# The first two batches of an attention kernel: clearing the key tiles with ScalarE, dropping four small transfers, splitting a weight semaphore

## Chip, cores and metric

The kernel runs on one core of one Trainium2 chip. The metric is the device time of one execution in microseconds (us); the number before the change is the median of three runs.

## What is computed

One cross-attention layer and one routed feed-forward layer, in float32:

```python
# x: (32, 256, 256), ctx: (32, 120, 256), 16 heads of 16
q = split(layernorm(x) @ Wq); k = split(ctx @ Wk); v = split(ctx @ Wv)
attn = softmax(q k^T * 16 ** -0.5)
x = x + (attn v) @ Wp + bp
# y = layernorm(x); each of 16 experts takes the 512 tokens with its highest router logit
xn = rmsnorm(y) * norm_weight
logits = xn @ router_weight.T + router_bias
idx = top_k(logits.T, 512)
h = gelu(xn[idx] @ fc1.T + b1); yo = h @ fc2.T + b2
out = x + (sum of gate * yo over experts) / (sum of gates)
```

## The kernel before

The program has an attention phase (32 batches, about the first 465 us) and a routed phase (the rest). The change touches the attention phase alone, and in it only what is done once, ahead of the loop or in its first steps.

**Attention phase.** Each of the five engines has a program of its own, built by a function `step(i, c)` and unrolled for the first steps, looped for the middle ones and unrolled for the last (`run`). In one step, different batches stand at different stages: an offset `off` in `batch(i, c, off)` names which. Batch b's keys, rows and queries are computed in step b-2, its row maxima in step b-1, its scores and weighted values in step b, its projection later. Semaphores join the engines; `wait_ge` on one stops all that stands behind it on that engine. The order of instructions on an engine is the order in which the code is written.

**Tiles for the exact products.** Queries and keys are split into a high and a low part (QH, QL, KH, KL), which are moved by DMA, interleaved by partition, into the wide tiles `QX[u]` and `KX[u]` (u is the batch's parity). One partition in 64 (`MAX_ROW` = 3 in each half) is the row that brings in the maxima: in QX it holds zeros first (from `no_max`) and later the negated row maxima (`NMT`), and in KX it holds ones. All partitions that no transfer writes must be zero. So before batch 0 and 1 both QX and both KX are cleared, and the two rows of ones in each KX are set.

**Who does that now.** VectorE clears `QX[0]` (L521) ahead of normalising the rows of batch 0 (L524, `first_rows`), and `KX[0]` (L527) behind it. GpSimd clears `QX[1]` and `KX[1]` (L362, L363, `zeros`) after it has computed the `rstd` of batch 0 (L342, L344). All four raise the one semaphore `zeros_ready`. GpSimd also fills `ones` (L331), and four transfers on SyncE's DMA queue (L219) copy it into the rows of KX; SyncE issues them only when `zeros_ready` has all four, and everything behind them on SyncE (the load of x for batch 2, then the transfers of `no_max`, KL, KH and QL of batch 0) waits too. TensorE's first row maxima (`max_scores`, L745) wait for `kx_moved`, `qx_moved` and `ones_moved`.

**TensorE at the start.** It multiplies the identity 12 times (`warm_up`, L664) while the weights come in, computes the keys of batch 0 (L688), transposes its rows (L674), computes its queries (L716), multiplies the identity 12 times more, and goes on with the keys of batch 1, the values of batch 0 (L731) and the row maxima. The queries of batch 0 wait for `w_loaded` at 16 * 7, which is all of wq, wv, wp, bp, nw, rw and rb.

Of the kernel before, what the change touches and what calls it, by code (L numbers as in the profile page):

```python
# [16 lines left out]
M = 120  # L17
# [21 lines left out]
NX = HN * HALVES  # L39
NCONST = 7  # L40
GMAX = float(CAP) - 0.5
ROUNDS = 8
CLOCK = 16
WARM = 12
ALONE = 2
# [3 lines left out]
FIRST_W1, FIRST_W2, SECOND_W1 = 3, 8, 20  # L49
FE = 2  # L50


# [8 lines left out]
def attention_phase(nc, ctx, sem, bank, ident, L, search_tiles, search_consts, x, ctxT, wq, wk, wv, wp, bp, nw, rw, rb, out, xn_table):  # L61
# [19 lines left out]
    no_max = sb("no_max", [H, S], FP32)  # L81
    ones = sb("ones", [1, H * M // HALVES], FP32)

# [42 lines left out]

    wk_loaded, w_loaded = sem("wk_loaded"), sem("w_loaded")
    x_loaded = [sem(f"x_loaded{u}") for u in range(2)]
# [6 lines left out]
    max_moved = [sem(f"max_moved{u}") for u in range(2)]  # L135
    ones_moved = sem("ones_moved")
    oc_moved, rc_moved = sem("oc_moved"), [sem(f"rc_moved{g}") for g in range(KD)]
    pool_const, zeros_ready, search_const = sem("pool_const"), sem("zeros_ready"), sem("search_const")
    stats1_a, stats1_ready = sem("stats1_a"), sem("stats1_ready")
# [18 lines left out]
    pool_passed, dve_passed, sp_passed = sem("pool_passed"), sem("dve_passed"), sem("sp_passed")  # L158
    CONSTS = 4

# [5 lines left out]
    def known(b):  # L166

        return isinstance(b, int)
# [26 lines left out]
    def _(sp):  # L195
# [9 lines left out]
        load_ctx(0, 0)  # L205
        for t, w, loaded in ((wk_sb, wk, wk_loaded), (wq_sb, wq, w_loaded), (wv_sb, wv, w_loaded), (wp_sb, wp, w_loaded)):
            sp.dma_start(t[:, :, :], w.rearrange("(k p) c -> p k c", p=P)).then_inc(loaded, 16)
# [6 lines left out]
        sp.wait_ge(pool_const, NCONST)  # L214
        sp.wait_ge(zeros_ready, CONSTS)
        for u in range(2):
            for f in range(HALVES):
                row = HP * f + MAX_ROW
                sp.dma_start(KX[u][row:row + 1, :, f, :, :].bitcast(FP32).rearrange("p n e m -> p n (e m)"),  # L219
                             ones[:, :].rearrange("p (n r) -> p n r", n=HN)).then_inc(ones_moved, 16)  # L220

# [5 lines left out]
        def step(i, c):  # L227
# [15 lines left out]
            def clear_maxima():  # L243
                b, u, j, live = batch(i, c, -2)
                if live:
                    hold(score_done, NX * (b - 1))
                    if known(b) and b < 2:
                        hold(zeros_ready, CONSTS)
                    sp.dma_start(QX[u][MAX_ROW:P:HP, :, :].bitcast(FP32), no_max[:, :]).then_inc(qx_moved[u], 16)
# [8 lines left out]
            def keys(term, part, ready):  # L258
                b, u, j, live = batch(i, c, -2)
                if live:  # L260
                    hold(ready, b + 1)
                    hold(score_done, NX * (b - 1))
                    if known(b) and b == 0:
                        hold(zeros_ready, CONSTS)
                    for f in range(HALVES):
                        sp.dma_start(KX[u][HP * f + term:HP * (f + 1):4, :, f, :, :].bitcast(FP32).rearrange("p n e m -> p n (e m)"),
                                     part[u][HP * f:HP * (f + 1), :, :].bitcast(FP32).rearrange("p e m -> p (e m)")) \
                            .then_inc(kx_moved[u], 16)
# [55 lines left out]
    def _(pool):  # L324
        pool.memset(ident[:, :], 0.0).then_inc(pool_const, 1)
        pool.wait_ge(pool_const, 1)
        pool.affine_select(out=ident[:, :], in_=ident[:, :], compare_op=ALU.not_equal, fill=1.0, base=0,
                           pattern=[[-1, P]], channel_multiplier=1).then_inc(pool_const, 1)
        pool.memset(minus_half[:, :], -0.5).then_inc(pool_const, 1)
        pool.memset(no_max[:, :], 0.0).then_inc(pool_const, 1)  # L330
        pool.memset(ones[:, :], 1.0).then_inc(pool_const, 1)  # L331
        for u in range(2):
            pool.memset(VA[u][:, :, :, :], 1.0).then_inc(pool_const, 1)
        pool.wait_ge(pool_const, NCONST)

        def step(i, c):
# [23 lines left out]

            def zeros():
                pool.memset(QX[1][:, :, :].bitcast(FP32), 0.0).then_inc(zeros_ready, 1)  # L362
                pool.memset(KX[1][:, :, :, :, :].bitcast(FP32), 0.0).then_inc(zeros_ready, 1)  # L363

            def rows1():
                b, u, j, live = batch(i, c, -2)
                if known(b) and b == 0:
                    zeros()
                elif live:
# [12 lines left out]
            def residual():  # L382
                b, u, j, live = batch(i, c, 1)
                if live:
                    if known(b) and b == 0:
                        pool.wait_ge(w_loaded, 16 * 7)
# [20 lines left out]
    @block.scalar  # L407
    def _(act):
        act.wait_ge(pool_const, NCONST)
        act.activation(warm[:, :], minus_half[:, 0:1], ACT.Exp)  # L410

        def step(i, c):
# [43 lines left out]
            def move_high(off, term):  # L456

                b, u, j, live = batch(i, c, off)
                if live:
                    act.wait_ge(qh_ready, b + 1)  # L460
                    if known(b) and b < 2:
                        act.wait_ge(zeros_ready, CONSTS)
# [18 lines left out]
            def rows2():  # L481
                b, u, j, live = batch(i, c, 3)
                if live:
                    act.wait_ge(xn2T_done, b + 1)
                    wait(act, logit_done, b - 1)
                    if known(b) and b == 0:
                        act.wait_ge(w_loaded, 16 * 7)
# [29 lines left out]
    @block.vector  # L517
    def _(dve):
        def step(i, c):
            def first_rows():  # L520
                dve.memset(QX[0][:, :, :].bitcast(FP32), 0.0).then_inc(zeros_ready, 1)  # L521
                dve.wait_ge(rstd1_ready, 1)
                for t in range(TB):
                    ins = dve.tensor_scalar(XN[0][:, t, :], X[0][:, t, :], mv1[0][:, t, 0:1], rstd1[0][:, t:t + 1],  # L524
                                            ALU.subtract, ALU.mult)
                ins.then_inc(xn_ready, 1)
                dve.memset(KX[0][:, :, :, :, :].bitcast(FP32), 0.0).then_inc(zeros_ready, 1)  # L527

# [131 lines left out]
    def _(pe):  # L660
# [5 lines left out]
        pe.wait_ge(pool_const, 2)  # L666
        warm_up(WARM)
        pe.wait_ge(wk_loaded, 16)

        def step(i, c):  # L670
# [63 lines left out]
            def max_scores(q):  # L734
                b, u, j, live = batch(i, c, -1)
                if live:
                    t, n = q // HN, q % HN
                    if q == 0:
                        if known(b) and b == 0:
# [105 lines left out]

            last = 2 * i + c - (B - 1) if known(i) else -B
            maxima()
            if last == 2:
# [5 lines left out]
            scores(1)  # L854
            values()
            scores(2)
            max_scores(0)
# [15 lines left out]
            max_scores(5)  # L873
            first = 2 * i + c if known(i) else 0
            if first != -1:
# [3 lines left out]
            if first == -1:  # L879
                queries()  # L880
            if first == -2:
                warm_up(WARM)
            weigh(2)
# [927 lines left out]
```

## Time and profile before

| what | value |
|---|---|
| median of 3 runs | 980.95 us (980.31 to 984.34) |
| the profiled execution's own time | 983.5 us |
| its span, first to last instruction | 981.8 us |
| PE, DVE, ACT, POOL busy | 861.1, 747.0, 505.8, 591.7 us |
| PE's share of the span | 88% |

PE is TensorE (PEld its weight loads), DVE VectorE, ACT ScalarE, POOL GpSimd, SP SyncE; SPq and ACTq are DMA instructions issued by SP and ACT. A float32 matmul leaves two records in the trace, so counts of PE are twice those of the program there. PEclk is the clock granted to TensorE, where 1.00 is 2.4 GHz and 0.50 is 1.2 GHz.

### The profile page before, as it was taken

To read this page: it belongs to the slowest core of one execution; us is meant where nothing else is said; L and a number is where in the kernel's file an instruction comes from. 1 tells how busy PE (TensorE), PEld (TensorE's weight loads), DVE (VectorE), ACT (ScalarE), POOL (GpSimd) and SP (SyncE) were. 2 spreads that over 40 slices of the span, in tenths; PEclk is the share of its full clock that TensorE was granted. 3 is DMA by queue.
4 is the path that set the end of the run, shared out by engine and by line. 5 is a ranking of instruction groups with operands and counts; after the bars stand their busy time and mean duration, and the time that the engine had idled before them with its cause. 6 is when DMAs were issued, how large, how long until landed. Compare 5 with 4: busy or idle time off the path is not lost. (4 is left out here: it accounts for less than half of the span.)

```text
span 981.8 us, 20963 instructions
## 1 busy us (share of the span) xinstructions
PE 861.1 (88%) x6115; PEld 737.1 (75%) x6115; DVE 747.0 (76%) x1660; ACT 505.8 (52%) x921; POOL 591.7 (60%) x564
## 2 busy tenths in 40 slices
PE   7899999999999999998711149999999999999995
PEld 6678887888788887886510037989999999999985
DVE  4488888888888888887388965898777777777642
ACT  1356556655566556655256206465555555555531
POOL 4256667666676667665442264688876776775344
PEclk8799999999999999999755559999999999999998
DMA  5266666666566656654232033366766555665333
GB/s 161 92 202 226 207 207 206 213 219 208 192 212 222 207 204 205 212 193 157 75 103 83 3 88 127 113 196 181 183 162 157 159 155 161 161 175 153 85 70 43
DMA packets 129540, 156.51 MB, mean 159 GB/s; under 512 B 22464, under 2 KB 104656, under 8 KB 129376
## 3 DMA queue, kind: packets, MB, share of 16 engines
q1 hardware_dynamic: 104096, 113.06, 35.5%
q0 software_dynamic: 15616, 25.70, 12.1%
q10 hardware_dynamic: 9792, 17.31, 4.8%
q8 instruction: 17, 0.28, 0.1%
q14 instruction: 19, 0.16, 0.1%
HBM read 74.93 MB, written 26.28 MB: 103 GB/s over the span
## 5 line engine op out<-in xcount | busy, mean ns | idle before, releaser
L587 DVE TENSOR_REDUCE NM<-bank 128x4 f32<-128x480 f32 x256 | 155.4, 649 | 59.9 <-PE bank L745 59.9
L418 ACT ACTIVATE PT<-bank 120x512 f32<-120x512 f32 x256 | 142.8, 603 | 35.9 <-PE bank L770 34.7
L349 POOL TENSOR_SCALAR XN<-X,mv,rstd 128x256 f32<-128x256 f32 x124 | 150.5, 1222 | 14.1 <-POOL rstd L344 13.3
L1658 PE MATMUL bank<-W2H,HH 128*128 128x256 f32 x512 | 145.5, 284 | 2.0 <-issue 2.0
L1660 PE MATMUL bank<-W2H,HL 128*128 128x256 f32 x512 | 144.3, 282 | 0.0
L1659 PE MATMUL bank<-W2L,HH 128*128 128x256 f32 x512 | 144.3, 282 | 0.0
L1119 POOL DMA_INDIRECT out_dram<-C,IO x60 | 109.6, 1827 | 52.2 <-issue 31.3
L1387 DVE TENSOR_TENSOR HL<-hf,HH 128x512 fp32r<-128x512 f32 x128 | 87.5, 691 | 49.8 <-ACT HH L1542 49.3
L545 DVE RECIPROCAL RR<-RC 128x256 f32<-128x256 f32 x64 | 111.6, 1743 | 8.6 <-DMA RC<-PVS 8.6
L770 PE MATMUL bank<-QX,KX 128*120 128x256 f32 x512 | 110.8, 309 | 8.2 <-DMA QX<-NMT 5.0
L1537 ACT ACTIVATE hf<-bank,B 128x512 f32<-128x512 f32 x128 | 87.8, 686 | 40.9 <-PE bank L1660 35.6
L342 POOL TENSOR_SCALAR ve<-mv 128x2 f32<-128x2 f32 x64 | 12.2, 191 | 159.4 <-DVE mv L535 156.7
L745 PE MATMUL bank<-KX,QX 128*128 128x240 f32 x512 | 103.0, 304 | 5.2 <-DMA QX<-QL 2.1
L1658 PEld LDWEIGHTS bank<-W2H,HH 128*128 128x128 f32 x512 | 97.3, 190 | 3.1 <-issue 2.4
L1658 PE MATMUL bank<-XTH,W1H 128*128 128x512 f32 x240 | 96.3, 401 | 2.9 <-DVE XTL L1380 2.9
L1659 PEld LDWEIGHTS bank<-W2L,HH 128*128 128x128 f32 x512 | 97.2, 190 | 0.6
L1660 PEld LDWEIGHTS bank<-W2H,HL 128*128 128x128 f32 x512 | 97.1, 190 | 0.0
L1530 ACT ACTIVATE W2H<-W 128x2048 fp32r<-128x2048 f32 x15 | 28.8, 1920 | 131.9 <-PE bank L1660 131.9
L1660 PE MATMUL bank<-XTH,W1L 128*128 128x512 f32 x240 | 95.1, 396 | 0.0
L1659 PE MATMUL bank<-XTL,W1H 128*128 128x512 f32 x240 | 95.0, 396 | 0.0
L745 PEld LDWEIGHTS bank<-KX,QX 128*128 128x128 f32 x512 | 76.5, 192 | 23.0 <-DVE NM L587 15.4
L1096 POOL DMA_INDIRECT XG<-xn_table,II x64 | 72.6, 1135 | 33.0 <-DVE out_row L1312 16.8
(194 smaller groups left out, 1906.6 us busy)
## 6 DMA issues: line engine op xcount, KB each, us to landing
QX<-QH ACTq DMA_DIRECT2D x64, 256.0 KB
W<-w1T_dram SPq DMA_DIRECT2D x16, 1024.0 KB, 5.3
W<-w2T_dram SPq DMA_DIRECT2D x16, 1024.0 KB, 5.9
X<-x_dram SPq DMA_DIRECT2D x32, 256.0 KB, 3.0
QX<-QL SPq DMA_DIRECT2D x32, 256.0 KB
XB<-x_dram SPq DMA_DIRECT2D x32, 256.0 KB, 2.8
RC<-PVS SPq DMA_DIRECT2D x64, 128.0 KB, 2.1
OC<-PVS SPq DMA_DIRECT2D x64, 128.0 KB, 2.2
```

The lines of the kernel that those rows point to most:

```text
L349: ins = pool.tensor_scalar(dst[:, t, :], src[:, t, :], mv[:, t, 0:1], rstd[:, t:t + 1], ALU.subtract, ALU.mult)
L418: act.activation(PT[u][0:M, HE * k:HE * (k + 1), :], score_bank(b, k // 2)[k % 2][0:M, :], ACT.Exp, scale=SCALE) \
L545: dve.reciprocal(RR[:, g, :], RC[:, g, :]).then_inc(rr_ready, 1)
L587: dve.tensor_reduce(NM[u][:, t, :].rearrange("p (f n e) -> p n e f", n=HN, e=HE)[:, n, :, :], smax_bank[q % 2][:, 0:4 * M].rearrange("p (e ...
L745: ins = pe.matmul(smax_bank[q % 2][:, e * 2 * M:(e + 1) * 2 * M], QX[u][:, HE * n + e, t * P:(t + 1) * P], KX[u][:, n, :, e, :], start=Tru ...
L770: ins = pe.matmul(score_bank(b, n)[f][0:M, e * S:(e + 1) * S], KX[u][:, n, f, e, :], QX[u][:, HE * n + e, :], start=True, stop=True)
L1119: pool.indirect_dma_start(out=out, in_=C[u][:, g, :], in_offset=None, compute_op=ALU.add, out_offset=bass.IndirectOffsetOnAxis(ap=IO[u][:, ...
L1387: dve.tensor_tensor(HL[u][:, f, :], HF[f % 4], HH[u][:, f, :].bitcast(FP32), ALU.subtract).then_inc(hl_ready, 1)
L1537: act.activation(HF[f % 4], h_bank[f % 4][:, :], ACT.Gelu, bias=B1[:, bass.ds(KF * e + f, 1)]).then_inc(hf_ready, 1)
L1658: pe.matmul(o, wh, xh, start=first, stop=False)
L1659: pe.matmul(o, wh, xl, start=False, stop=False)
L1660: return pe.matmul(o, wl, xh, start=False, stop=last)
```

## The change

- ScalarE clears both KX and sets their rows of ones in the same operation: eight activations (four per tile), each writing 480 elements per partition as a tile of ones (`VA[0]`) times a column of the identity, which is 1 in partition `MAX_ROW` of a half and 0 elsewhere. They stand ahead of everything else on ScalarE.
- The four transfers of ones, the tile `ones`, its memset and the semaphore `ones_moved` are gone, as are the memsets of KX on VectorE and GpSimd.
- VectorE clears `QX[0]` as its first instruction. GpSimd clears `QX[1]` in its preamble, ahead of the `rstd` of batch 0, and fills the two VA tiles sooner.
- `zeros_ready` is split into `qx_cleared[u]` and `kx_cleared[u]`, so each transfer waits only for its own tile.
- The queries of batch 0 wait for wq alone (`wq_loaded`); the wait for the other weights stands ahead of the values.
- The second warm-up of 12 becomes 4 ahead of the queries of batch 0, and 8 ahead of the first row maxima.

```diff
-NCONST = 7
+NCONST = 6
-WARM = 12
+WARM = 12, 4, 8
@@ sync
-        for t, w, loaded in ((wk_sb, wk, wk_loaded), (wq_sb, wq, w_loaded), ...
+        for t, w, loaded in ((wk_sb, wk, wk_loaded), (wq_sb, wq, wq_loaded), ...
         sp.wait_ge(pool_const, NCONST)
-        sp.wait_ge(zeros_ready, CONSTS)
-        for u in range(2):
-            for f in range(HALVES):
-                row = HP * f + MAX_ROW
-                sp.dma_start(KX[u][row:row + 1, :, f, :, :]..., ones[:, :]...).then_inc(ones_moved, 16)
@@ clear_maxima
-                        hold(zeros_ready, CONSTS)
+                        hold(qx_cleared[u], 1)
@@ keys
-                    if known(b) and b == 0:
-                        hold(zeros_ready, CONSTS)
+                    if known(b) and b < 2:
+                        hold(kx_cleared[u], 1)
@@ gpsimd
+        for u in range(2):
+            pool.memset(VA[u][:, :, :, :], 1.0).then_inc(pool_const, 1)
         pool.memset(minus_half[:, :], -0.5).then_inc(pool_const, 1)
         pool.memset(no_max[:, :], 0.0).then_inc(pool_const, 1)
-        pool.memset(ones[:, :], 1.0).then_inc(pool_const, 1)
-        for u in range(2):
-            pool.memset(VA[u][:, :, :, :], 1.0).then_inc(pool_const, 1)
+        pool.memset(QX[1][:, :, :].bitcast(FP32), 0.0).then_inc(qx_cleared[1], 1)
         pool.wait_ge(pool_const, NCONST)
...
-            def zeros():
-                pool.memset(QX[1][:, :, :].bitcast(FP32), 0.0).then_inc(zeros_ready, 1)
-                pool.memset(KX[1][:, :, :, :, :].bitcast(FP32), 0.0).then_inc(zeros_ready, 1)
@@ scalar
+        act.wait_ge(pool_const, 3)
+        for u in range(2):
+            for f in range(HALVES):
+                row = HP * f + MAX_ROW
+                for n in range(0, HN, 2):
+                    ins = act.activation(KX[u][:, n:n + 2, f, :, :],
+                                         VA[0][:, 0:HE * 2 * M // (DH * 2), :, :].rearrange("p h d o -> p (h d o)")
+                                         .rearrange("p (n e m) -> p n e m", n=2, e=HE), ACT.Copy, scale=ident[:, row:row + 1])
+            ins.then_inc(kx_cleared[u], 1)
         act.wait_ge(pool_const, NCONST)
         act.activation(warm[:, :], minus_half[:, 0:1], ACT.Exp)
@@ vector
+        dve.memset(QX[0][:, :, :].bitcast(FP32), 0.0).then_inc(qx_cleared[0], 1)
...
-                dve.memset(QX[0][:, :, :].bitcast(FP32), 0.0).then_inc(zeros_ready, 1)
                 dve.wait_ge(rstd1_ready, 1)
...
-                dve.memset(KX[0][:, :, :, :, :].bitcast(FP32), 0.0).then_inc(zeros_ready, 1)
@@ tensor, queries
-                        pe.wait_ge(w_loaded, 16 * 7)
+                        pe.wait_ge(wq_loaded, 16)
@@ values
+                    if known(b) and b == 0:
+                        pe.wait_ge(w_loaded, 16 * 6)
@@ max_scores
-                        if known(b) and b == 0:
-                            pe.wait_ge(ones_moved, 16 * 2 * HALVES)
@@ step
             values()
+            if first == -1:
+                warm_up(WARM[2])
...
+            if first == -2:
+                warm_up(WARM[1])
             if first != -1:
                 queries()
...
-            if first == -2:
-                warm_up(WARM)
```

On TensorE, the first instructions of the program before (ident is the identity, XN the normalised rows, XNT their transpose):

```order
L664 MATMUL bank<-ident 128x128 x12
L688 MATMUL bank<-CTX,wk_sb 128x120 x4
L674 MATMUL bank<-ident,XN 128x128 x4
L716 MATMUL bank<-XNT,wq_sb 128x256 x4
L664 MATMUL bank<-ident 128x128 x12
L688 MATMUL bank<-CTX,wk_sb 128x120 x4
L731 MATMUL bank<-wv_sb,CTX 120x256 x2
L745 MATMUL bank<-KX,QX 128x240 x4
L674 MATMUL bank<-ident,XN 128x128 x4
```

and of the changed one, four lines of the file earlier:

```order
L660 MATMUL bank<-ident 128x128 x12
L684 MATMUL bank<-CTX,wk_sb 128x120 x4
L670 MATMUL bank<-ident,XN 128x128 x4
L660 MATMUL bank<-ident 128x128 x4
L712 MATMUL bank<-XNT,wq_sb 128x256 x4
L684 MATMUL bank<-CTX,wk_sb 128x120 x4
L729 MATMUL bank<-wv_sb,CTX 120x256 x2
L660 MATMUL bank<-ident 128x128 x8
L741 MATMUL bank<-KX,QX 128x240 x4
```

Four of the twelve products now stand ahead of the queries and eight between the values and the first row maxima.

On SyncE, the instructions behind the loads of the weights, before:

```order
L213 DMA rb_sb<-rb_dram 128x16
L219 DMA KX<-ones 1x4x240 [waits zeros_ready,pool_const]
L219 DMA KX<-ones 1x4x240 x3
L197 DMA X<-x_dram 128x2x256 [waits xn_ready]
L249 DMA QX<-no_max 2x8x256 [waits zeros_ready]
L266 DMA KX<-KL 16x4x240 [waits zeros_ready,kl_ready]
```

and now:

```order
L212 DMA rb_sb<-rb_dram 128x16
L196 DMA X<-x_dram 128x2x256 [waits xn_ready,pool_const]
L242 DMA QX<-no_max 2x8x256 [waits qx_cleared0]
L259 DMA KX<-KL 16x4x240 [waits kx_cleared0,kl_ready]
L259 DMA KX<-KL 16x4x240
```

The four transfers and the wait for all four clears are gone; the tile of batch 0 alone is waited for.

On ScalarE, the start before:

```order
L410 ACT_TABLE_LOAD
L410 ACTIVATE warm<-minus_half 128x1 [waits pool_const]
L479 ACTIVATE KH<-bank 128x240 [waits k_done]
L434 ACTIVATE XNT<-bank 128x512 [waits xnT_done]
L454 ACTIVATE QH<-bank 128x512 [waits q_done]
```

and now:

```order
L401 ACT_TABLE_LOAD
L401 ACTIVATE KX<-VA,ident 128x2x240 [waits pool_const]
L401 ACTIVATE KX<-VA,ident 128x2x240 x7
L406 ACTIVATE warm<-minus_half 128x1 [waits pool_const]
L475 ACTIVATE KH<-bank 128x240 [waits k_done]
L430 ACTIVATE XNT<-bank 128x512 [waits xnT_done]
```

Eight activations now stand ahead of the eviction of batch 0's keys.

## Rows read from the trace of the kernel before

**Rows 1.** Timeline of ScalarE: start us, us, instruction, idle before; evictions of the maxima

```profile
33.46 0.37 ACT L443 ACTIVATE NMT<-bank 16x256 fp32r<-16x256 f32 x1 [0.61 <-ACT QH L454]
...
48.83 0.36 ACT L443 ACTIVATE NMT<-bank 16x256 fp32r<-16x256 f32 x1
...
61.93 0.36 ACT L443 ACTIVATE NMT<-bank 16x256 fp32r<-16x256 f32 x1
```

**Rows 2.** Timeline of all engines, 0 to 14.5 us

```profile
1.61 5.17 PE L664 MATMUL bank<-ident 128*128 128x128 f32 x24 [1.61 <-POOL minus_half L329]
...
2.64 0.98 POOL L333 MEMSET VA<- 128x512 f32 x2
...
5.15 0.73 POOL L344 TENSOR_TENSOR rstd<-ve,minus_half 128x2 f32<-128x2 f32 x1
...
6.62 1.05 PE L688 MATMUL bank<-CTX,wk_sb 128*128 128x120 f32 x8
...
7.71 0.37 ACT L479 ACTIVATE KH<-bank 128x240 fp32r<-128x240 f32 x1 [3.85 <-PE bank L688]
...
9.79 1.11 PE L674 MATMUL bank<-ident,XN 128*128 128x128 f32 x4 [2.12 <-DVE XN L524]
...
10.95 0.60 ACT L434 ACTIVATE XNT<-bank 128x512 f32<-128x512 f32 x1 [2.87 <-PE bank L674]
...
11.69 3.75 PE L716 MATMUL bank<-XNT,wq_sb 128*128 128x256 f32 x8 [0.78 <-ACT XNT L434]
11.83 2.63 SPq L219 DMA_DIRECT2D KX<-ones  x4
```

**Rows 3.** Instructions of line 524: ns min/median/max, first and last start us

```profile
L524 DVE TENSOR_SCALAR XN<-X,mv,rstd x2: 395/1545/2695, 6.7 to 9.3; 128x256 f32<-128x256 f32 x2
```

**Rows 4.** Timeline of all engines, 15 to 23 us

```profile
15.23 3.48 PE L664 MATMUL bank<-ident 128*128 128x128 f32 x24
...
15.70 1.27 SPq L266 DMA_DIRECT2D KX<-KL  x2
16.10 1.29 ACTq L189 DMA_DIRECT2D QX<-QH  x2
16.11 0.69 DVE L554 TENSOR_TENSOR QL<-bank,QH 128x512 fp32r<-128x512 f32 x1 [3.05 <-ACT QH L454]
17.06 2.89 SPq L266 DMA_DIRECT2D KX<-KH  x4
...
20.00 0.59 SPq L189 DMA_DIRECT2D QX<-QL  x1
...
22.53 0.69 PE L745 MATMUL bank<-KX,QX 128*128 128x240 f32 x4 [2.07 <-DMA QX<-QL]
```

**Rows 5.** Timeline of TensorE, 28 to 45 us

```profile
28.59 3.63 PE L716 MATMUL bank<-XNT,wq_sb 128*128 128x256 f32 x8
...
37.01 1.21 PE L770 MATMUL bank<-QX,KX 128*120 128x256 f32 x4 [2.96 <-DMA QX<-NMT]
...
44.94 1.89 PE L716 MATMUL bank<-XNT,wq_sb 128*128 128x256 f32 x8
```

**Rows 6.** Windows of 2 us: length, busy (count) by engine, PEclk, DMA share, GB/s

```profile
16.00:18.00 2.00, 2.00 (x18) 2.00 (x17) 0.69 (x1) 0.07 (x1) 0.89 (x1) 0.86 0.73 254
...
24.00:26.00 2.00, 1.81 (x7) 1.40 (x7) 1.69 (x4) 0.43 (x1) 0.00 (x0) 0.50 0.12 33
```

**Rows 7.** ScalarE by line and shape, whole kernel: count, busy us, mean ns

```profile
L489 ACT ACTIVATE XN2T<-bank,nw_sb 128x256 f32<-128x256 f32 x64 | 26.7, 474 | 17.9 <-PE bank L674 17.9
...
L472 ACT ACTIVATE VA<-bank 120x256 f32<-120x256 f32 x32 | 12.7, 398 | 2.0 <-PE bank L731 1.7
```

**Rows 8.** Timeline of GpSimd, 5.5 to 10 us: its two memsets

```profile
5.84 1.79 POOL L362 MEMSET QX<- 128x2048 f32 x1
...
7.58 1.69 POOL L363 MEMSET KX<- 128x1920 f32 x1
```

**Rows 9.** DMA issues by line, 0 to 60 us: KB each, us to landing

```profile
rb_sb<-rb_dram SPq DMA_DIRECT2D x1, 8.0 KB, 3.5
```

More of the change, by code:

```diff
@@ L81, in attention_phase @@
     no_max = sb("no_max", [H, S], FP32)
-    ones = sb("ones", [1, H * M // HALVES], FP32)
     X = pair("X", [P, TB, D], FP32)
@@ L125, in attention_phase @@
     query_bank, xn2_bank = bank[7], bank[7]
-    wk_loaded, w_loaded = sem("wk_loaded"), sem("w_loaded")
+    wk_loaded, wq_loaded, w_loaded = sem("wk_loaded"), sem("wq_loaded"), sem("w_loaded")
     x_loaded = [sem(f"x_loaded{u}") for u in range(2)]
@@ L135, in attention_phase @@
     max_moved = [sem(f"max_moved{u}") for u in range(2)]
-    ones_moved = sem("ones_moved")
+    qx_cleared = [sem(f"qx_cleared{u}") for u in range(2)]
+    kx_cleared = [sem(f"kx_cleared{u}") for u in range(2)]
     oc_moved, rc_moved = sem("oc_moved"), [sem(f"rc_moved{g}") for g in range(KD)]
-    pool_const, zeros_ready, search_const = sem("pool_const"), sem("zeros_ready"), sem("search_const")
+    pool_const, search_const = sem("pool_const"), sem("search_const")
     stats1_a, stats1_ready = sem("stats1_a"), sem("stats1_ready")
@@ L158, in attention_phase @@
     pool_passed, dve_passed, sp_passed = sem("pool_passed"), sem("dve_passed"), sem("sp_passed")
-    CONSTS = 4
     def wait(eng, s, value):
@@ L205, in _ @@
         load_ctx(0, 0)
-        for t, w, loaded in ((wk_sb, wk, wk_loaded), (wq_sb, wq, w_loaded), (wv_sb, wv, w_loaded), (wp_sb, wp, w_loaded)):
+        for t, w, loaded in ((wk_sb, wk, wk_loaded), (wq_sb, wq, wq_loaded), (wv_sb, wv, w_loaded), (wp_sb, wp, w_loaded)):
             sp.dma_start(t[:, :, :], w.rearrange("(k p) c -> p k c", p=P)).then_inc(loaded, 16)
@@ L214, in _ @@
         sp.wait_ge(pool_const, NCONST)
-        sp.wait_ge(zeros_ready, CONSTS)
-        for u in range(2):
-            for f in range(HALVES):
-                row = HP * f + MAX_ROW
-                sp.dma_start(KX[u][row:row + 1, :, f, :, :].bitcast(FP32).rearrange("p n e m -> p n (e m)"),
-                             ones[:, :].rearrange("p (n r) -> p n r", n=HN)).then_inc(ones_moved, 16)
         def hold(s, value):
@@ L359, in attended @@
                     pool.tensor_tensor(OT[u][:, :, :], OC[:, :, :], RR[:, :, :], ALU.mult).then_inc(oT_ready, 1)
-            def zeros():
-                pool.memset(QX[1][:, :, :].bitcast(FP32), 0.0).then_inc(zeros_ready, 1)
-                pool.memset(KX[1][:, :, :, :, :].bitcast(FP32), 0.0).then_inc(zeros_ready, 1)
             def rows1():
                 b, u, j, live = batch(i, c, -2)
-                if known(b) and b == 0:
-                    zeros()
-                elif live:
+                if live and not (known(b) and b == 0):
                     wait(pool, xnT_done, b - 1)
@@ L385, in residual @@
                     if known(b) and b == 0:
-                        pool.wait_ge(w_loaded, 16 * 7)
+                        pool.wait_ge(w_loaded, 16 * 6)
                     pool.wait_ge(xb_loaded[u], 16 * (j + 1))
@@ L461, in move_high @@
                     if known(b) and b < 2:
-                        act.wait_ge(zeros_ready, CONSTS)
+                        act.wait_ge(qx_cleared[u], 1)
                     if off == -2:
@@ L486, in rows2 @@
                     if known(b) and b == 0:
-                        act.wait_ge(w_loaded, 16 * 7)
+                        act.wait_ge(w_loaded, 16 * 6)
                     for k in range(KD):
@@ L666, in _ @@
         pe.wait_ge(pool_const, 2)
-        warm_up(WARM)
+        warm_up(WARM[0])
         pe.wait_ge(wk_loaded, 16)
@@ L738, in max_scores @@
                     if q == 0:
-                        if known(b) and b == 0:
-                            pe.wait_ge(ones_moved, 16 * 2 * HALVES)
                         pe.wait_ge(kx_moved[u], 16 * 6 * (j + 1))
@@ L846, in step @@
             last = 2 * i + c - (B - 1) if known(i) else -B
+            first = 2 * i + c if known(i) else 0
             maxima()
@@ L873, in step @@
             max_scores(5)
-            first = 2 * i + c if known(i) else 0
+            if first == -2:
+                warm_up(WARM[1])
             if first != -1:
@@ L880, in step @@
                 queries()
-            if first == -2:
-                warm_up(WARM)
             weigh(2)
```

## The prediction

> **What bounds the kernel now.** I read the page first: TensorE is busy 88% of the span, but that is an average, and the change touches only work of the first two batches. So I asked whether a shift there reaches the end. The timeline of ScalarE has one eviction of the maxima per batch: 33.46, 48.83 and 61.93 us [rows 1], steps of 15.4 and 13.1 us. Nothing in the program waits for a fixed time; loops follow each other through semaphores. A microsecond won before the scores of batch 0 (37.01 us [rows 5]) is one won at the end, unless the first steps lose it again.
>
> Then I followed the start with the timeline. Batch 0 goes keys, transposes, queries, moves, row maxima. Four waits stand out.
> - TensorE ends its keys at 7.67 and starts the transposes at 9.79, waiting for XN [rows 2]. VectorE's two operations on XN took 2.695 and 0.395 us, though they are the same shape [rows 3]. The long one lasts from 6.7 to about 9.4; GpSimd's two memsets fill 5.84 to 9.27 [rows 8].
> - The queries take 3.75 us [rows 2], where the same line takes 1.89 at 44.94 [rows 5].
> - SyncE issues nothing until 11.83, then the ones for 2.63 us, KL at 15.70, KH from 17.06 to 19.95, and QL only at 20.00, although QL was computed at 16.80 [rows 2, 4].
> - The first row maxima start at 22.53, released by the transfer of QL, 2.53 us after its issue; TensorE sat idle 2.07 us [rows 4]. By 24 to 26 the granted clock is 0.50 (1.2 GHz) [rows 6]; the queries of batch 1 then take 3.63 us [rows 5].
>
> **The change, step by step.** All times are on the trace's clock.
>
> *XN.* `rstd` ends at 5.88 [rows 2]. GpSimd's preamble loses `ones` and gains QX[1] (1.79 us [rows 8]); VA ended at 3.62 before [rows 2], so with `ones` gone (0.9 us less) it ends at about 4.5 to 4.8, when the statistics of batch 0 are ready anyway (`rstd` starts 5.15): cost nothing, 0.2 at most. VectorE's clear of QX[0] ends before x has landed: nothing either. No memset of GpSimd then lies beside XN, so it costs 2 x 0.395: ready at 6.8 instead of 9.74, before the keys end at 7.67. The transposes start at 7.7 instead of 9.79, a gain of 2.1.
>
> What if the 2.695 us is XN's own start-up and not the memsets' doing? Then XN is ready at 5.95 + 2.70 + 0.40 = 9.05 and the sum loses 1.3 us. I take 0.395, since the second operation started when the last memset had ended. The Trainium skill (SBUF — State Buffer, Who interferes with whom) says that VectorE and GpSimd share a port pair and that a `tensor_scalar` in a fast two-port mode blocks fully until the other is done; by that rule the sum is the one I take, and these rows agree with it (2.695 against 0.395 us).
>
> *ScalarE.* Eight activations of 480 elements from when VA[0] is filled, 1.61 + 0.49 = 2.1 [rows 2]; the table load stood ahead of the wait before too. No such operation is in the trace. Evictions of 240 and 512 elements took 0.37 and 0.60 [rows 2], which puts 480 at 0.57; a scale read from a tile adds 474 - 398 = 76 ns at 256 elements [rows 7]. Lower bound 0.57, 0.65 likely, upper bound 0.474 x 480/256 = 0.89. So they end at 6.7, 7.3 or 9.2, and the 0.2 us Exp behind them. What is queued behind is KH of batch 0, at 7.71: no cost at 0.65, up to 1.7 us at 0.89 (by way of KL, and SyncE behind KL). Unlike the rest of this edit's cover, this slack of 0.2 is thin.
>
> *TensorE.* Transposes 7.7 to 8.3 (half of 1.11, the clock being still up), XNT 0.60 more: 8.95. Four identity products: the first 12 cost 5.17 us [rows 2], the second 12 cost 3.48, of which the clock was up for the later part (a mean of 0.86 over 16 to 18) [rows 4, 6]. With the clock up one costs about half of 0.43, so four end at 9.2. rb, the last of the weights, was issued as the twelfth transfer, near 6.4, and took 3.5 us [rows 9]: 9.9. With the old wait the queries would start there, so `wq_loaded` (eight issues sooner, landed near 6) is worth 0.7 here; before, it would have been worth nothing, since XNT came later. Queries 9.2 to 11.1 at 1.89 [rows 5] instead of 15.44. TensorE never stops between 1.61 and there, so I take the fast price. Keys of batch 1 take 1.05 [rows 2], the values, half as many products of twice the columns, about the same: 13.2; rb is there. Eight identity products: 14.9.
>
> *The moves.* QH and QL cost 0.6 and 0.7: QL is ready at 12.5. SyncE: x of batch 2 and `no_max` from 6.9 to 8.0, KL when computed (KH 7.71 + 0.37 + 0.4 = 8.5) to 9.8, KH to 12.7, QL at 12.8 instead of 20.00. Landing 2.5 later gives 15.3. But the two QH transfers (256 KB each) are issued at 11.8 to 13.1 and share the engines with QL: From 16 to 18 the engines moved 254 GB/s at a share of 0.73 [rows 6], so 350 at full share; 768 KB and some KH from 13.1 on end near 15.7. I take 15.8 for the first row maxima; the range is 15.3 to 16.5. The gain at this point is 22.53 - 15.8 = 6.7 us.
>
> *Up to the scores.* From the first maxima to the queries of batch 1 is 28.59 - 22.53 = 6.06 us [rows 4, 5], set by VectorE's eight reductions as much as by TensorE; unchanged, the queries start at 21.9. Before the maxima TensorE now idles 0.9 us, not 2.07. If the clock stays up they cost 1.89 instead of 3.63: 23.8 against 32.22, a gain of 8.5. From there to the scores, 32.22 to 37.01, it is ScalarE's evictions, its queue and a transfer: 4.8 us unchanged, so scores start at 28.5. The idle time ahead of them is as long as before, so I count no gain on their clock.
>
> The sum: the end of batch 0's queries moves from 15.44 to 11.1, -4.3 (XN 2.1, the transposes' faster clock 0.5, the queries' 1.9, less what the four products add beyond XNT, 0.2); SyncE, which made QL wait 3.2 us (16.80 to 20.00) and now 0.3, would give 2.9 more, of which sharing with QH takes 0.5: -6.7 at the maxima; batch 1's queries -1.8: **-8.5 us**. Against the profiled execution's 983.5 that is 975.0; that execution lay 2.5 above the median of 980.95, for which it gives 972.5.
>
> **The rivals.**
> - *A, as above, clock up through batch 1's queries:* 972.5 us. For it: idle time before falls of the clock was 2.1 us or more here. Against: TensorE is only some 60% busy through the maxima, as VectorE's reductions pace it.
> - *B, the clock falls during the maxima all the same:* -6.7 us, 974.3. For it: 0.50 over 24 to 26 [rows 6], with the maxima under way.
> - *C, a loss at the head:* the clear ends late (up to 1.7), XN keeps its 2.7 (1.3), or the clock is down through queries, keys and values. That last is the dearest: transposes to 8.8, XNT 9.5, identity to 11.2, queries to 14.9, keys and values to 18.4, eight identity products at 0.43 to 21.9, which is 0.6 before 22.53. C spans 974 to 980.4. Against it: before, the keys ran at 1.05 us [rows 2], the fast price, once the first warm-up was over. The Trainium skill (TensorE: Matmul & The Clock Gate, What's actually happening) has it that sustained activity releases the throttle and idleness restores it, at a moment that varies between runs; by that rule it is A or B here, and the first warm-up's slow pace and the keys' fast one agree.
> - *D, no change:* the lead is given back in the first steps, because batch 1 and 2 are bound by something unshifted. For it: the first step is 15.4 us, not 13.1. Against: that step's excess is the slow clock at 37.01, and every wait in it hangs on the same chain. 981.
> - *E, slower:* ScalarE's clears hold up the keys' eviction. Batch 0 keeps a gain until they end 8.5 us late, at about 16, that is 1.7 us each; for 5 us slower they would need 2.4 each. My upper bound is 0.89. At 2.4 each: 986.
>
> **How the numbers follow.** Chances: A 0.42, B 0.28, C 0.14, D 0.11, E 0.05. About 0.5%, or 4.9 us, is what a measurement of this kernel can tell from no change, so faster means below 976.0: A, B and a third of C, 0.75. Same: the rest of C and D, 0.20. Slower 0.05. The prediction is A's 972.5; A's own range is 970.5 to 974 (landing of QL 15.3 to 16.5, and the transfer of the maxima, which took 3.15 us from issue to scores and might take 1 less). The whole range takes in B and most of C: 970 to 978.
>
> **What would show it.** XN at 0.4 us twice; ScalarE's eight clears at 0.6 to 0.7, ending before 7.5; transposes at 7.7; queries of batch 0 in 1.9 us from 9.2; SyncE's QL at 12.8; first row maxima near 15.8; queries of batch 1 in 1.9 us; scores at 28.5; from there the same step times. The prediction is wrong if the scores' start moves by another amount than 6.7 to 8.5, or if it moves so and the end doesn't follow.

## The result

The changed kernel takes 975.01 us (median of 7 runs, 970.46 to 977.46), the kernel before in the same comparison 983.9 us (7 runs, 978.94 to 985.87). The ratio is 0.9912, with a 95% interval of 0.9893 to 0.9932: about 8.7 us faster (the two medians lie 8.9 apart), more than the 0.5% that tells it from no change. The forecast was 8.5 us and 972.5; the gain was met, and the absolute time came out 2.5 higher because the three runs shown before had a median of 980.95, 2.95 below the 983.9 of seven.

The profiled execution took 970.46 us (span 968.7, granted clock 0.941), the fastest of the seven. Here is the timeline of its head, all engines (start us, us, instruction, idle before and its releaser):

```profile
1.62 4.63 PE L660 MATMUL bank<-ident 128*128 128x128 f32 x24 [1.62 <-POOL ident L320]
2.12 4.80 ACT L401 ACTIVATE KX<-VA,ident 128x480 fp32r<-128x480 f32 x8
...
5.98 0.74 DVE L521 TENSOR_SCALAR XN<-X,mv,rstd 128x256 f32<-128x256 f32 x2 [1.24 <-POOL rstd L337]
6.08 1.05 PE L684 MATMUL bank<-CTX,wk_sb 128*128 128x120 f32 x8
...
6.97 0.60 PE L670 MATMUL bank<-ident,XN 128*128 128x128 f32 x4
7.17 0.37 ACT L475 ACTIVATE KH<-bank 128x240 fp32r<-128x240 f32 x1 [0.15 <-PE bank L684]
...
8.16 1.24 SPq L259 DMA_DIRECT2D KX<-KL  x2
8.35 1.97 PE L712 MATMUL bank<-XNT,wq_sb 128*128 128x256 f32 x8
9.50 2.45 SPq L259 DMA_DIRECT2D KX<-KH  x4
...
10.98 0.69 DVE L550 TENSOR_TENSOR QL<-bank,QH 128x512 fp32r<-128x512 f32 x1
11.99 0.60 SPq L188 DMA_DIRECT2D QX<-QL  x1
12.34 1.95 PE L660 MATMUL bank<-ident 128*128 128x128 f32 x16
...
15.38 0.69 PE L741 MATMUL bank<-KX,QX 128*128 128x240 f32 x4 [1.10 <-DMA QX<-QL]
...
20.89 1.89 PE L712 MATMUL bank<-XNT,wq_sb 128*128 128x256 f32 x8
24.03 0.37 ACT L439 ACTIVATE NMT<-bank 16x256 fp32r<-16x256 f32 x1 [0.61 <-ACT QH L450]
27.57 0.73 PE L766 MATMUL bank<-QX,KX 128*120 128x256 f32 x4 [3.69 <-DMA QX<-NMT]
38.28 0.36 ACT L439 ACTIVATE NMT<-bank 16x256 fp32r<-16x256 f32 x1
```

Against [rows 2, 4, 5]: XN costs 0.74 us for both operations, the transposes start at 6.97 instead of 9.79, QL goes out at 11.99 instead of 20.00, the first row maxima start at 15.38 instead of 22.53, the queries of batch 1 take 1.89 instead of 3.63, and the scores start at 27.57 instead of 37.01. The second eviction of the maxima comes at 38.28 instead of 48.83 [rows 1], 10.55 us sooner.

The clock shows why the last part is quick. The windows of the changed kernel (length, busy of PE, PEld, DVE, ACT, POOL, PEclk, DMA share, GB/s):

```profile
14.00:18.00 4.00, 2.55 (x16) 1.77 (x15) 2.10 (x4) 0.60 (x1) 0.76 (x1) 1.00 0.61 192
18.00:22.00 4.00, 2.75 (x14) 2.04 (x15) 3.59 (x9) 0.00 (x0) 2.12 (x4) 1.00 0.24 78
22.00:26.00 4.00, 1.89 (x14) 1.50 (x12) 0.69 (x1) 0.97 (x2) 1.22 (x2) 1.00 0.33 122
26.00:30.00 4.00, 2.17 (x13) 1.86 (x14) 0.41 (x1) 2.25 (x5) 0.00 (x0) 1.00 0.64 210
```

From the first keys on, at 6.08 us, the clock is never at its lower level in the head of this execution, though TensorE is busy for 2.75 of 4 us during the maxima and 1.89 of 4 before the scores. Ahead of that PEclk reads 1.00 too, but can't be trusted there: the first 12 products took 0.39 us each (4.63 in all), and the eight from 12.34 on 0.24 each.

### The profile page after: what moved, and what is told of

It reads as the page before. It is cut to its first block and busy times, and to the rows that moved or that the text cites. A ratio compares the mean times of both kernels' runs of the same rounds, so it can differ in the third digit from the quotient of the medians.

```text
span 968.7 us, 20968 instructions
## 1 busy us (share of the span) xinstructions
PE 848.8 (88%) x6115; PEld 727.1 (75%) x6115; DVE 742.9 (77%) x1659; ACT 510.7 (53%) x929; POOL 594.6 (61%) x562
```

## The experiments

Each number below is on the trace's clock of one profiled execution. "First maxima" is the start of the row maxima of batch 0, "scores" the start of its scores, and "second eviction" the second eviction of the maxima, from which on the attention phase takes 410.9 to 413.1 us to its last one in every kernel here. So the second eviction tells what a change in the head is worth. The column "first 12" is the time that the first 12 identity products took, the same instructions in every kernel. The five kernels with one thing taken back or made worse, and the kernel before with one gap filled, ran once each, so only their traces are read here.

| kernel | first 12 | first maxima | scores | second eviction | span |
|---|---|---|---|---|---|
| before | 5.17 | 22.53 | 37.01 | 48.83 | 981.8 |
| changed | 4.63 | 15.38 | 27.57 | 38.28 | 968.7 |
| changed, once more | 5.39 | 16.10 | 29.61 | 41.07 | 974.1 |
| changed, no later identity products | 5.12 | 16.10 | 30.70 | 42.30 | 974.5 |
| changed, queries wait for all weights | 4.38 | 19.49 | 33.61 | 45.84 | 979.7 |
| changed, with the transfers of ones | 4.47 | 17.87 | 32.31 | 44.06 | 975.4 |
| changed, clears in small pieces | 5.49 | 19.74 | 33.49 | 45.00 | 977.7 |
| changed, QX[1] cleared beside XN | 5.49 | 16.85 | 30.32 | 41.71 | 975.8 |
| changed, gaps filled | 5.18 | 15.90 | 28.14 | 38.96 | 969.9 |
| before, one gap filled | 4.64 | 23.49 | 37.60 | 49.82 | 982.5 |
| before, gaps filled | 5.49 | 23.40 | 36.19 | 46.78 | 979.5 |
| changed, maxima ahead of queries | 5.08 | 15.93 | 26.78 | 39.12 | 969.7 |
| the same, gaps filled | 4.77 | 15.62 | 24.91 | 38.88 | 970.0 |

The first 12 products took 4.38 to 5.49 us. What stands behind them moves along: in the repetition they took 0.76 us more than in the first profile of the changed kernel, and keys, transposes and row maxima began 0.76, 0.76 and 0.72 later. So the first profile is an early one, and up to 0.9 us of a delay against it may be no doing of the edit.

**GpSimd's clear beside XN.**

```diff
-        pool.memset(QX[1]...).then_inc(qx_cleared[1], 1)    # preamble
+                if known(b) and b == 0:                      # rows1, behind rstd
+                    pool.memset(QX[1]...).then_inc(qx_cleared[1], 1)
```

> The changed kernel with GpSimd's clear of QX[1] back behind the rstd of batch 0, beside VectorE's XN. Theory 1 (GpSimd's memset blocks the tensor_scalar of VectorE): the first of the two operations on XN takes about 1.7 to 1.8 us instead of 0.37, and XN is ready near 8.1 instead of 6.72. Since the transposes wait at 6.97, the queries and the maxima come about 1.1 us later. Theory 2 (the 2.695 us had another cause): both operations stay at 0.4 us and nothing moves.

The timelines of its VectorE and GpSimd:

```profile
6.03 2.19 DVE L522 TENSOR_SCALAR XN<-X,mv,rstd 128x256 f32<-128x256 f32 x2 [1.24 <-POOL rstd L336]
...
5.96 1.79 POOL L356 MEMSET QX<- 128x2048 f32 x1
```

and line 522 by itself (ns min/median/max):

```profile
L522 DVE TENSOR_SCALAR XN<-X,mv,rstd x2: 395/1134/1874, 6.0 to 7.8; 128x256 f32<-128x256 f32 x2
```

The two operations take 2.19 us instead of 0.74. The first took 1.874 us and ended at 7.9, as the memset did (7.75) but for 0.15, and the second took 0.395, so the first one was stopped until the memset had ended. The memset itself is no slower. The Trainium skill (SBUF — State Buffer, Who interferes with whom) has this as an exclusive lock on a shared port pair; these runs agree (2.19 against 0.74 us). What this cost the kernel is another matter. The maxima start 1.5 us later than in the first profile and the second eviction comes 3.4 later, but TensorE itself was late here:

```profile
6.90 1.34 PE L685 MATMUL bank<-CTX,wk_sb 128*128 128x120 f32 x8
8.28 0.66 PE L671 MATMUL bank<-ident,XN 128*128 128x128 f32 x4
```

Its first 12 products took 5.49 us, so its keys ended at 8.24, when XN was ready as well (8.22). Against the repetition, which had the same late start (5.39) and no memset beside XN, the maxima are 0.75 later and the second eviction 0.64. The blocking is shown by this run; a cost of 3.4 us is not.

**The transfers of ones.**

```diff
         sp.wait_ge(pool_const, NCONST)
+        for u in range(2):
+            sp.wait_ge(qx_cleared[u], 1)
+            sp.wait_ge(kx_cleared[u], 1)
+        (the four transfers of ones, as before)
```

> The changed kernel with the four transfers of ones back at their old place in SyncE's program (ones over ones, so nothing else changes), behind a wait for all four clears. Theory 1 (SyncE's queue was the larger part of the gain at the maxima): the transfers go out from about 7.0 to 9.6, KL then from 10.8 instead of 8.16, QL from 14.6 instead of 11.99, and the first maxima start near 18.0 instead of 15.38. Theory 2 (the queue had slack): the maxima move by less than 1 us.

The timeline of SyncE's queue:

```profile
7.12 2.64 SPq L222 DMA_DIRECT2D KX<-ones  x4
9.80 0.45 SPq L198 DMA_DIRECT2D X<-x_dram  x1
10.29 0.58 SPq L252 DMA_DIRECT2D QX<-no_max  x1
10.99 1.27 SPq L269 DMA_DIRECT2D KX<-KL  x2
12.37 2.83 SPq L269 DMA_DIRECT2D KX<-KH  x4
15.24 0.60 SPq L190 DMA_DIRECT2D QX<-QL  x1
```

Four transfers of 3.8 KB hold SyncE for 2.64 us, and QL goes out 3.25 later than in the changed kernel; the maxima start at 17.87, 2.5 later. The queue was the path. This run puts back the transfers, and not the late clears: in the kernel before SyncE was held until 11.83, as VectorE's clear of KX[0] ended at 11.75, where here it starts at 7.12. What taking that clear off VectorE is worth has no run of its own.

**One semaphore for all weights.**

```diff
                         pe.wait_ge(wq_loaded, 16)
+                        pe.wait_ge(w_loaded, 16 * 6)
```

> The changed kernel, but the queries of batch 0 wait for all seven weights again. Theory 1 (the split semaphore is worth what it lets start sooner): the queries of batch 0 start near 9.9 instead of 8.35, QL is ready near 13.2 instead of 11.67, and the first maxima start near 16.8 instead of 15.38. Theory 2 (the maxima are bound by the transfers of KL and KH, the queries' parts come in their shadow): the maxima move by less than 0.5 us.

The timeline of TensorE:

```profile
7.30 1.06 PE L660 MATMUL bank<-ident 128*128 128x128 f32 x8
10.96 3.26 PE L713 MATMUL bank<-XNT,wq_sb 128*128 128x256 f32 x8 [2.60 <-DMA rb_sb<-rb_dram]
...
19.49 0.69 PE L742 MATMUL bank<-KX,QX 128*128 128x240 f32 x4 [1.36 <-DMA QX<-QH]
```

The last weight came at 10.9, not 9.9 (4.5 us from issue here, 3.5 before [rows 9]), and TensorE idled 2.60 us. The queries started 2.6 us later than in the changed kernel: the 0.7 that I had priced, 1.1 by the weight's later landing, and 0.8 because without the wait they were ready at 8.35 and not at 9.2. It cost more than that wait: the queries then took 3.26 instead of 1.97, and the second eviction came 7.6 us later.

**The clears in small pieces.**

```diff
-                for n in range(0, HN, 2):   (one activation of 480 elements)
+                for n in range(HN):
+                    for e in range(HE):     (one activation of 120 elements)
```

> The changed kernel with ScalarE's clears of KX in 32 pieces of 120 elements instead of 8 of 480. Theory 1 (the clears have almost no slack before the eviction of the keys of batch 0): at about 0.27 us each they end near 10.7 instead of 6.92, the eviction of the keys starts near 10.9 instead of 7.17, and the first maxima come about 3.2 us later, near 18.6. Theory 2 (they are off the path, as the queries' moves end last): the maxima stay within 1 us of 15.4.

The timeline of ScalarE:

```profile
2.12 9.24 ACT L402 ACTIVATE KX<-VA,ident 128x120 fp32r<-128x120 f32 x32
11.26 0.19 ACT L407 ACTIVATE warm<-minus_half 128x1 f32<-128x1 f32 x1
11.35 0.35 ACT L476 ACTIVATE KH<-bank 128x240 fp32r<-128x240 f32 x1
```

A piece took 0.29 us, and everything behind it slid: the eviction of the keys starts 4.2 us later and the maxima 4.4, and the clears end 4.4 later (11.36 against 6.92). So there was little slack: in the changed kernel's first profile ScalarE is idle for 0.15 us between its Exp behind the clears and the eviction, which TensorE releases; in the repetition, with its later keys, for 0.91.

**The later identity products, taken out** (`WARM = 12, 0, 0`).

> The changed kernel without its four and eight identity products (the first twelve stay). Theory 1 (the products keep the clock): TensorE idles from 12.5 to 15.4 ahead of the first maxima, the clock falls, the queries of batch 1 take 3.6 us and the scores start near 29.3, not 27.57. Theory 2 (the shorter chain alone keeps the clock up): queries at 1.9 us; the queries of batch 0 start 0.15 earlier and the scores at 27.4 to 27.6.

```profile
14.00:18.00 4.00, 1.90 (x10) 1.93 (x11) 1.22 (x2) 0.14 (x1) 0.64 (x1) 0.81 0.75 248
18.00:22.00 4.00, 2.86 (x11) 2.18 (x10) 3.26 (x9) 0.46 (x1) 0.97 (x3) 0.50 0.23 77
22.00:26.00 4.00, 4.00 (x12) 3.01 (x13) 1.20 (x2) 0.04 (x1) 2.36 (x2) 0.50 0.01 4
```

These are the windows of this kernel. TensorE stood idle for 3.55 us ahead of the maxima, the clock fell with them, batch 1's queries took 3.63 us, and the second eviction came at 42.30. That is 4.0 later than in the changed kernel's first profile and 1.2 later than in its second one, below, where the clock fell too. So what the products do for the clock is seen, and their worth in time isn't clear of what one program varies by.

**The changed kernel once more, and with its gaps filled.**

```diff
+            if first == 0:              # behind keys(), ahead of scores(0)
+                warm_up(12)
...
+            if first == -1: warm_up(1)  # behind max_scores 2, 3 and 4
+            if first == -1: warm_up(5)  # behind max_scores 5
```

> The changed kernel with 20 more identity products where TensorE idles in the head: one each behind the third, fourth and fifth row maxima of batch 0, five behind the sixth, and twelve behind the keys of batch 2 ahead of the scores of batch 0. They cost TensorE about 0.24 us each with the clock up and lie in idle time. Theory 1 (the runs of the changed kernel fall into groups near 970.5 and 975 because the clock falls in the head in some of them): with the gaps filled the clock stays up in the head in every run, the median is 970 to 972, and no run is above 973. Theory 2 (the groups come from the later phases): the spread stays 970 to 977 and the median 974 to 975.

> The changed kernel once more, unchanged, beside the filled one on the same chip. Theory 1 (the clock's state in the head differs from run to run): the medians stand 2 us or more above the filled kernel's, with single runs near 970.5 and others near 975, and a profile may show the clock at 0.50 during the maxima or the first scores. Theory 2: medians within 1 us of each other.

The repetition gave 975.45 us (6 runs, 972.61 to 976.74; ratio 0.9921, 0.99 to 0.9942), and the windows of its profile show what the first profile did not:

```profile
18.00:22.00 4.00, 2.63 (x11) 1.99 (x12) 3.54 (x9) 0.00 (x0) 1.40 (x3) 0.80 0.22 70
22.00:26.00 4.00, 3.84 (x19) 3.08 (x17) 1.36 (x3) 0.61 (x2) 1.94 (x2) 0.77 0.05 15
26.00:30.00 4.00, 0.39 (x3) 0.39 (x4) 0.51 (x2) 0.73 (x2) 0.00 (x0) 1.00 0.80 256
30.00:34.00 4.00, 4.00 (x19) 3.57 (x18) 1.26 (x2) 2.86 (x6) 0.00 (x0) 0.58 0.32 106
```

The same program, and the clock falls under the queries of batch 1 and again under the first scores. The maxima start 0.7 later than in the first profile, as the first 12 products took 0.76 longer, and the second eviction comes 2.8 later. The Trainium skill (TensorE: Matmul & The Clock Gate, What's actually happening) says that the moment of a change varies from run to run, as the monitor's window doesn't start with the kernel; two profiles of one program that differ so agree with it.

The filled kernel took 973.55 us (6 runs, 970.5 to 975.71; ratio 0.9911, 0.9886 to 0.9936). Its profile has the clock at 1.00 from 6 to 50 us, yet its runs still lie near 971 (three) and 975.5 (three). So the expectation that the spread would go with the head's clock failed, at least in part, and the two medians, 1.9 us apart with overlapping intervals, decide between neither pair of theories. A second source is in the profiles at the other end. From the first product of the first expert to the end, seven of the thirteen take 391.8 to 393.3 us and six 394.2 to 395.0; of these six, five show a mean clock of 0.91 in one 20 us stretch near the end, where the others have 1.00. The windows of the kernel before and of the changed one there, both 350 to 370 us behind the first product of the experts (length, PE busy, PEclk, DMA share, GB/s):

```profile
937.00:957.00 20.00, 18.77 (x121) 0.91 0.39 86
```

```profile
925.80:945.80 20.00, 18.93 (x129) 1.00 0.38 86
```

The code of this stretch is the same in both kernels. Counted from the first product of the experts, ScalarE's work ahead of it lies 0.2 us later in the kernel before and behind it 1.7 us, so it made 1.5 of the 13.1 us between the two spans. The lower clock shows there in the kernel before and in four variants of the changed one, so it doesn't come with one of the two kernels; what brings it on is not shown. Whether it explains the filled kernel's two groups I can't say: only one of its runs has a trace.

**The clock alone, on the kernel before.** First with eight products ahead of the first maxima, then with the other 20 as well.

> The kernel before, with eight more identity products between the values and the first row maxima of batch 0, where TensorE idled 2.07 us. Theory 1 (the clock is a gain of its own, apart from the shorter chain): the clock stays at 1.00 through the maxima, the queries of batch 1 take 1.9 us, not 3.63, and the scores of batch 0 start near 35.2, not 37.01; the first maxima stay at 22.5. Theory 2 (the clock stays up only because the whole head is continuous): it falls all the same, the queries take 3.6 us, and the scores stay near 37.

> The kernel before with 28 more identity products: the eight ahead of the first row maxima and the 20 of the filled kernel. Theory 1 (the clock in the head is worth about 3 us by itself, and the earlier fall came in the unfilled maxima): the queries of batch 1 take 1.9 us, not 3.63, the first scores step takes 14.3 instead of 15.4 us, and the second eviction of the maxima comes near 46.5 instead of 48.83; the median falls by 2 to 3 us, the rest of the changed kernel's gain staying away. Theory 2 (the products delay what they stand before): the second eviction comes at 48.8 or later.

The first failed as an experiment. The products ended at 21.14, but QL went out 0.9 us later than in the kernel before, as KL and KH held SyncE for 5.2 us instead of 4.3, and the maxima started at 23.49, so a gap of 2.35 us stayed ahead of them, as long as the one it was to fill; the clock fell during the maxima and batch 1's queries took 3.51. It tells nothing of a filled gap. In the second the same gap stays, the clock is 0.50 over 26 to 28, but the products among the maxima bring it back by 29, and the timeline of TensorE has

```profile
29.48 1.89 PE L716 MATMUL bank<-XNT,wq_sb 128*128 128x256 f32 x8
...
36.19 0.73 PE L770 MATMUL bank<-QX,KX 128*120 128x256 f32 x4 [1.03 <-DMA QX<-NMT]
```

and the second eviction 2.05 us earlier; the median was 981.23 (12 runs; ratio 0.9987, 0.9972 to 1.0001). What these products did for the clock is thus worth 2 us in the profile (2.9 from the first maxima on, which started 0.9 later for the same delay of QL), and the time is not clear of noise.

**Maxima ahead of the queries of batch 1**, without and with eight products in the gaps of the maxima. Both change the order of two pieces on TensorE and on ScalarE; the second adds the products.

```diff
-            if first == -1:
-                queries()              # step -1, behind max_scores(7)
+            maxima()
+            if first == 0:
+                queries(-1)            # step 0
```

> The changed kernel with the queries of batch 1 computed and evicted behind the transpose and eviction of the maxima of batch 0, on TensorE and ScalarE. Theory 1 (the queries of batch 1 stand between the maxima and the scores of batch 0): the maxima are evicted near 22.4 instead of 24.03, the scores start near 25.9 instead of 27.57, and a median about 1.7 us lower than the changed kernel's, which is inside the noise of a single comparison. Theory 2 (the gain is given back, as the scores of batch 1 wait for the queries' moves): the second eviction of the maxima stays near 38.3.

> The kernel that evicts the maxima of batch 0 ahead of the queries of batch 1, with eight identity products in the idle time between the row maxima (one each behind the third, fourth and fifth, five behind the sixth). Theory 1 (its lead of 1.4 us at the scores is given back since batch 1's own row maxima wait for the moves of QH and QL, which now come later): with the clock up the queries of batch 1 take 1.9 us and the scores start near 26, but the second eviction of the maxima stays at 38.5 to 39.2. Theory 2 (it was given back because the clock fell under its queries): the second eviction comes near 37.4, and the median near 971.

They took 972.83 us (6 runs, 971.39 to 975.16; ratio 0.9905, 0.9886 to 0.9924) and 973.0 (6 runs, 971.7 to 974.79; ratio 0.9906, 0.9889 to 0.9923), medians 2 us below the changed kernel's; but each was measured beside its own runs of the kernel before, and by the ratios they are 0.6 to 1.6 us below it, with intervals that overlap its own. In the first the clock fell under batch 1's queries, which took 3.02 us, and the scores started at 26.78. The timeline of the second:

```profile
22.47 0.37 ACT L439 ACTIVATE NMT<-bank 16x256 fp32r<-16x256 f32 x1 [5.09 <-PE bank L759]
...
24.91 0.73 PE L771 MATMUL bank<-QX,KX 128*120 128x256 f32 x4
...
25.55 0.55 SPq L188 DMA_DIRECT2D QX<-QL  x1
27.05 0.49 PE L771 MATMUL bank<-QX,KX 128*120 128x256 f32 x2 [0.54 <-DMA QX<-QL]
29.07 0.49 PE L746 MATMUL bank<-KX,QX 128*128 128x240 f32 x2 [1.52 <-issue]
```

The scores start at 24.91, 2.7 us before those of the changed kernel, and the second eviction at 38.88, 0.6 after its 38.28. The row maxima of batch 1 start at 29.07 instead of 29.66, so 2.1 of the 2.7 us are lost there. They need all of batch 1's transfers, and the last of these is issued hardly sooner: QL at 25.55 here, and in the changed kernel the second transfer of QH at 25.64 (QL went at 24.17). In both kernels with this order the row maxima begin 3.52 us after QL's issue. The rest goes under a clock that was 0.65 over 30 to 34, which this experiment doesn't separate from the order. That the lead is given back within one step is shown by both kernels; starting the scores early brings little if the next batch's operands don't come early too.

## Why the prediction was right, point by point

- **XN:** 0.74 us for both, ready at 6.72 (predicted 6.8). That GpSimd's memset was the cause is shown by putting one back. The 2.1 us that I counted for it is TensorE's idle time in the kernel before (2.12), and no other run confirms that price.
- **ScalarE's clears:** 0.60 us each, ended at 6.92 (predicted 0.65 and 7.3). That they had little slack is shown (0.15 us in the first profile, 0.91 in the repetition).
- **TensorE:** keys began at 6.08, not 6.62, since the first 12 products took 4.63 us instead of 5.17; the transposes at 6.97, not 7.7; the queries took 1.97 from 8.35 (predicted 1.9 from 9.2). The fast price held. The early start was luck: in the repetition the 12 took 5.39, the keys began at 6.84 and the transposes at 7.73, as forecast.
- **The moves:** SyncE sent QL at 11.99 (12.8); it was there 3.4 us later, at 15.38 (15.8), which is 0.9 longer than in the kernel before. I had allowed 0.5 for sharing with QH. Five profiles bear the sharing out: where QL went 3.9 us behind the first transfer of QH it took 2.53 us (before) and 2.63 (with the transfers of ones), at 1.6 behind 3.04 (no later products), at 1.0 behind 3.39, and at 0.9 behind 3.50 (the repetition). The gain at the maxima was 7.15 us, predicted 6.7; in the repetition 6.4.
- **Up to the scores:** 27.57, predicted 28.5: a gain of 9.4 against 8.5 in the profiled run. By my own sign (a move of 6.7 to 8.5) the first profile is a miss, and the repetition, with 7.4, is not. Of the 0.9 too much, 0.4 came at the maxima, by the lucky start, and 0.55 behind them: the row maxima, which I had left at 6.06 us up to batch 1's queries, took 5.51 with the clock up. The 4.8 from these queries to the scores held (4.79).
- **Mis-sized, the first step:** I counted no gain on the clock between the scores and the second eviction. It took 10.7 us instead of 11.8 in this execution, 1.1 more; in the repetition 11.5. Against D I had said that the first step's 15.4 us, 2.3 above the next, were the slow clock. With the clock up all through, the step still took 14.25 (24.03 to 38.28) against 13.09 for the next, so the clock was half of it; what the other half is stays open.
- **Mis-sized, `wq_loaded`:** 0.7 by my working, 4.1 at the maxima and 7.6 at the second eviction when taken away. I had priced the wait with a later start of the queries and an earlier landing of rb than came, and not what the idle TensorE does to the clock behind it. The sum was not touched, as it took the wait as gone.
- **A or B:** these are not two outcomes of the change but of a run. The first profile is A; the repetition has the clock falling during batch 1's queries, as B said, with a gain at the scores of 7.4 and at the second eviction of 7.8. The ratio's 8.7 lies between the head's 7.8 and 10.55. That it falls so near my 8.5 is partly luck: neither profile gained 8.5, the absolute median of 975.01 lies outside A's own range and nearer to B's 974.3, and the head of the kernel before is known from one profile.
- **D and E:** from the second eviction to the last, 411.7 us before and 411.9 after, so the lead was kept. The two profiles' spans differ by 13.1: 10.55 in the head, -0.2 in the rest of the attention, 0.9 up to the experts, and 1.9 behind their first product, of which 1.5 under the lower clock near the end.

The parts' worth at the second eviction holds only as far as one program repeats itself there (38.28 and 41.07, 2.8 us). Against the first profile and against the repetition it is 7.6 and 4.8 for the split semaphore, 5.8 and 3.0 for the transfers of ones, 4.0 and 1.2 for the products, and 3.4 and 0.6 for the memset away from XN. So the first is clear of that spread, the second just so, and the last two are not. Against the first profile they sum to more than the 10.55 of all together. In each of these runs the clock falls between the first maxima and the end of batch 1's queries, so part of each figure is likely the clock's, counted again each time; no run separates it.

## What to carry to other kernels

In the head of a kernel, before the pipeline is full, one late operand can cost its wait and then again what TensorE's clock loses by it (here a wait of 2.6 us became 7.6, or 4.8 against the repetition); price both, and look at how long TensorE runs at its lower level in the trace. Small transfers are paid for by the queue that issues them: a constant that an idle engine could write took 2.64 us of SyncE's time here as four tiny DMAs in front of the ones that mattered. A profile is one execution: where the clock is near the edge, take a second one before a difference of 3 us is read from it, and look first at what ran ahead of the edit: here the same 12 products differed by up to 1.1 us.

## What the runs showed of the hardware

- A memset on GpSimd held up VectorE's `tensor_scalar` for its whole length (the first of two operations took 2.695 us before and 1.874 with one memset put back, about 0.4 without), while two memsets, one on each engine, ran side by side at full pace: 1.76 us on VectorE from 1.32, with GpSimd filling VA in 0.98 from 1.52, as long as in the kernel before, beside a VectorE that was idle but for the last 0.1 us.
- The clock's falls did not follow the longest idle stretch. In the repetition of the changed kernel it had fallen to 0.50 by 20.5 us, after idle stretches of 1.50 and 1.10 us with 2.63 of 4 us busy around them; in the first profile of that same program it stayed at 1.00 through 3.69 us of idle time before the scores.
- The first 12 products of the program took 4.38 to 5.49 us in thirteen profiles, and in the changed kernel TensorE's next work (keys, transposes, maxima) moved with them.
- A 256 KB transfer had landed 2.53 to 2.63 us after its issue (when the row maxima that waited for it began) when it went 3.9 us behind the first of two others of its size, and after 3.39 to 3.50 when it went about 1 us behind that one.
- ScalarE's activation cost 0.60 us for 480 elements and 0.29 for 120, so most of a small one does not depend on its size.
